# Adjacency counts in groups of 10 targets with three edge chunks, and attention denominators of four chunks summed in eight partitions

## The reference, cut to what matters

```
edge_index = stack([src, dst]); xn = layernorm(x)
# graph layer
norm = dinv[src] * dinv[dst]                       # dinv = 1 / sqrt(degree)
gnn  = relu(segment_sum((xn @ W)[src] * norm[:, None], dst) + b)
# linear attention, 16 heads of 64
phiQ, phiK = elu(Q) + 1, elu(K) + 1
S     = einsum('bhki,bhkj->bhij', phiK, V);  Z = phiK.sum(-2)
denom = einsum('bhqi,bhi->bhq', phiQ, Z)[..., None] + 1e-6
mix   = (einsum('bhqi,bhij->bhqj', phiQ, S) / denom) @ Wo.T + bo
x = x + gnn + mix
x = x + ffn(layernorm(x))                          # ternary weights, silu, two gelu layers
```

## Time and profile before

| | |
|---|---|
| median of 3 runs | 996.22 us (995.83 to 997.37) |
| the profiled execution: its own time | 995.84 us |
| its span in the trace | 994.1 us |
| TensorE busy | 975.2 us, 98% of the span |
| VectorE busy | 543.9 us, 55% |
| ScalarE busy | 293.6 us, 30% |
| GpSimd busy | 142.4 us, 14% |
| granted TensorE clock | 0.999 |

### The profile page before, as it was taken

The page is one execution under the profiler, slowest core; times in us unless marked ns, Lnnn a source line. Parts: engine busy times, 40 slices in busy tenths (PEclk is TensorE's granted clock), DMA queues, the critical chain, the costliest instruction groups (busy, mean ns, idle before and its releaser), DMA issues.

```text
span 994.1 us, 13325 instructions
## 1 busy us (share of the span) xinstructions
PE 975.2 (98%) x4860; PEld 824.4 (83%) x4860; DVE 543.9 (55%) x1067; ACT 293.6 (30%) x585; POOL 142.4 (14%) x191
## 2 busy tenths in 40 slices
PE   5999999999999999999999999999999999999998
PEld 4887888888889989978786788767788999999986
DVE  6886578777763888782113556447557212122354
ACT  6873122232133343341213221114113312135300
POOL 7101001001011050050300000000201103064100
PEclk9999999999999999999999999999999999999999
DMA  7412013113021022122201465535422302010053
GB/s 269 150 49 86 5 30 117 28 31 100 16 77 36 26 90 73 52 69 95 96 12 55 147 204 172 157 119 186 170 80 90 123 1 85 1 43 1 22 190 139
DMA packets 46979, 86.78 MB, mean 87 GB/s; under 512 B 19036, under 2 KB 23388, under 8 KB 46896
## 3 DMA queue, kind: packets, MB, share of 16 engines
q1 hardware_dynamic: 38416, 57.28, 17.5%
q0 software_dynamic: 8480, 28.45, 8.7%
HBM read 61.62 MB, written 24.09 MB: 86 GB/s over the span
## 4 chain that ended last, share of the span: by engine, by line
PE 92%; DVE 3%; DMA 2%; ACT 1%; issue 1%; POOL 1%; SPq 0%; DVEq 0%; ACTq 0%; POOLq 0%
PE PS L1431 11%; PE PS L1433 11%; PE PS L1432 11%; PE PS L1552 9%; PE PS L1553 9%; PE PS L1554 9%; PE PS L1610 5%; PE PS L1612 4%; PE PS L1630 3%; PE PS L1631 3%; PE PS L1629 3%; PE PS L1471 2%; PE PS L1446 2%; PE PS L1683 2%; PE PS L1682 2%; PE PS L1681 2%
## 5 line engine op out<-in xcount | busy, mean ns | idle before, releaser
L1431 PE MATMUL PS<-ring,act_t 128*128 128x512 f32 (+1 forms) x480 | 194.7, 406 | 1.3 <-POOL ring L443 0.6
L1433 PE MATMUL PS<-ring,act_t 128*128 128x512 f32 (+1 forms) x480 | 190.7, 397 | 0.0
L1432 PE MATMUL PS<-ring,act_t 128*128 128x512 f32 (+1 forms) x480 | 190.3, 396 | 0.0
L1552 PE MATMUL PS<-act_t,ring 128*128 128x416 f32 (+1 forms) x432 | 159.3, 369 | 1.4 <-POOL ring L443 1.3
L1553 PE MATMUL PS<-act_t,ring 128*128 128x416 f32 (+1 forms) x432 | 152.2, 352 | 0.0
L1554 PE MATMUL PS<-act_t,ring 128*128 128x416 f32 (+1 forms) x432 | 151.7, 351 | 0.0
L1431 PEld LDWEIGHTS PS<-ring,act_t 128*128 128x128 f32 (+1 forms) x480 | 89.8, 187 | 23.9 <-POOL ring L443 1.6
L1433 PEld LDWEIGHTS PS<-ring,act_t 128*128 128x128 f32 (+1 forms) x480 | 89.5, 186 | 22.4
L1432 PEld LDWEIGHTS PS<-ring,act_t 128*128 128x128 f32 (+1 forms) x480 | 89.9, 187 | 21.2 <-issue 0.5
L1552 PEld LDWEIGHTS PS<-act_t,ring 128*128 128x128 f32 x432 | 81.3, 188 | 6.8 <-issue 3.4
L1553 PEld LDWEIGHTS PS<-act_t,ring 128*128 128x128 f32 x432 | 81.4, 188 | 4.0 <-issue 3.4
(11 more groups left out here) (195 smaller groups left out, 1650.7 us busy)
## 6 DMA issues: line engine op xcount, KB each, us to landing
stage_x<-in_wslices_dram POOLq DMA_DIRECT2D x54, 256.0 KB, 4.2
stage<-in_wslices_dram POOLq DMA_DIRECT2D x42, 256.0 KB, 3.7
xr<-x_d SPq DMA_DIRECT2D x18, 512.0 KB, 3.6
phin_d<-phiq SPq DMA_DIRECT2D x8, 625.0 KB, 3.1
xrow<-in_x_dram SPq DMA_DIRECT2D x9, 512.0 KB, 3.6
xh<-in_x_dram SPq DMA_DIRECT2D x18, 256.0 KB
x_d<-xh SPq DMA_DIRECT2D x18, 256.0 KB
x_d<-xr SPq DMA_DIRECT2D x9, 512.0 KB, 3.0
```

Source lines behind the costliest of these rows:

```text
L1431: pe.matmul(out_ap, node_rows(0, k, t), ring[:, slot(k0 + k), 0, :], start=(k == 0), stop=False)
L1432: pe.matmul(out_ap, node_rows(1, k, t), ring[:, slot(k0 + k), 0, :], start=False, stop=False)
L1433: ins = pe.matmul(out_ap, node_rows(0, k, t), ring[:, slot(k0 + k), 1, :], start=False, stop=(k == KD - 1))
L1552: pe.matmul(out_ap, w[0], x_t[:, 0, k, o:o + n], start=(k == 0), stop=False)
```

## The change

There are two parts.

**Counts.** Groups have 10 targets (`WIN` 13 to 10) and three chunks (`STATIC_CHUNKS` 4 to 3). The first nine tiles then have 13 groups and the last has 10: 127 groups where there were 100. Two groups of a tile that stand beside each other are worked on as a pair (`PARTS`, 68 of them; a tile's thirteenth group stands alone): one pass of VectorE for each of the two arrays, six matmuls into one bank, one copy by ScalarE. Three parts are done in a step, in steps 12 to 34. The array buffers go from 5 to 4 (`OH_BUFS`). The key loads stay one for each group.

**Denominators.** The queries are done in another order (`q_chunk`: for a half of the features, four blocks `f` of one chunk of nodes one after the other). Such a group of four units has its denominators in one PSUM bank, in eight partitions: two heads for each of four units. `z_hl` and `phi_hl` are high and low fp32r parts, so a unit takes three fp32r matmuls with 8 columns of weights (`denominator`), for which ScalarE makes the high part (`phi_split`) and VectorE the low part (`phi_rest`). Once in four units ScalarE copies 8 partitions (`den_copy`) and VectorE inverts them (`den_invert`). SyncE writes them to DRAM (`rec_d`) and reads them back into all 128 partitions, 64 for each head (`rec_spread`). VectorE multiplies unit `i - 8` in its turn `i` (`PHI_LAG`), and each unit is stored by itself.

The core of the diff:

```
-STATIC_CHUNKS = 4
+STATIC_CHUNKS = 3
...
-OH_BUFS = 5
+OH_BUFS = 4
 KEY_BUFS = 4
-WIN = 13
+WIN = 10
...
-PHI_BUFS = 3
+PHI_BUFS = 9
+PHI_LAG = 8
...
+def q_chunk(i):
+
+    s, r = divmod(i, 12)
+    return 4 * s + r % 4, r // 4
...
+def groups_of(t):
+
+    return -(-rows(t) // WIN)
+
+
+PARTS = [(t, j, min(2, groups_of(t) - j)) for t in range(NT) for j in range(0, groups_of(t), 2)]
+
+
 def windows_of(step):
 
-    if 12 <= step < 37:
-        return list(range(4 * (step - 12), 4 * (step - 11)))
+    if 12 <= step < 35:
+        return list(range(3 * (step - 12), min(3 * (step - 11), len(PARTS))))
     return []
...
+            def phin_store(i):
+                f, c = q_chunk(i)
+                o, n = CHUNKS[c]
+                sp.wait_ge(phin_ready, i + 1)
+                sp.dma_start(phin_d[f, :, o:o + n], phiq[:, i % PHI_BUFS, 0:n]).then_inc(phin_stored[i % PHI_BUFS], 16)
+
+            def rec_spread(g):
+                n = CHUNKS[g % 3][1]
+                sp.wait_ge(rec_ready, g + 1)
+                sp.dma_start(rec_d[g].rearrange("a b n -> (a b) n")[:, 0:n], rec[0:8, 0:n]).then_inc(rec_stored, 16)
+                sp.wait_ge(rec_stored, 16 * (g + 1))
+                sp.wait_ge(phin_ready, 4 * g)
+                for h in range(2):
+                    sp.dma_start(rec_all[64 * h:64 * h + 64, :, 0:n],
+                                 rec_d[g, :, h, 0:n].unsqueeze(0).to_broadcast([64, 4, n])).then_inc(rec_in, 16)
...
-                for j in range(WPT):
+                for j in range(groups_of(dt)):
                     w = WPT * dt + j
                     first = sp.value_load(bounds[0:1, w:w + 1], min_val=0, max_val=LAST_FIRST)
...
-                if step >= 40 and (step - 40) % 3 == 2 and (step - 40) // 3 >= 1:
-                    phin_store((step - 40) // 3 - 1)
-            phin_store(KD - 1)
+            for i in range(24 + PHI_LAG):
+                if i >= PHI_LAG:
+                    phin_store(i - PHI_LAG)
+                if 7 <= i < 28 and i % 4 == 3:
...
+            def den_copy(g):
+                n = CHUNKS[g % 3][1]
+                act.wait_ge(phi_used, 4 * (g + 1))
+                if g >= 1:
+                    act.wait_ge(rec_stored, 16 * g)
+                nc.scalar.activation(rec[0:8, 0:n], PS[0:8, 3 + g % 2, 0:n], ACT.Identity,
+                                     bias=eps_sb[0:8]).then_inc(den_read, 1)
+
+            def phi_split(i):
+                n = CHUNKS[q_chunk(i)[1]][1]
+                act.wait_ge(phiq_ready, i + 1)
                 if i >= 2:
-                    act.wait_ge(phin_ready, i - 1)
-                nc.scalar.activation(rec[:, i % 2, 0:n], PS[:, 3 + i % 2, 0:n], ACT.Identity,
-                                     bias=eps_sb).then_inc(den_read, 1)
+                    act.wait_ge(phi_used, i - 1)
+                nc.scalar.activation(phi_hl[:, 0, i % 2, 0:n], phiq[:, i % PHI_BUFS, 0:n], ACT.Copy).then_inc(phi_hi, 1)
...
             def window(w):
-                dt, j = divmod(w, WPT)
+                dt, j, m = PARTS[w]
                 b = w % OH_BUFS
...
+            def phi_rest(i):
+                n = CHUNKS[q_chunk(i)[1]][1]
+                dve.wait_ge(phi_hi, i + 1)
+                dve.tensor_tensor(phi_hl[:, 1, i % 2, 0:n], phiq[:, i % PHI_BUFS, 0:n],
+                                  phi_hl[:, 0, i % 2, 0:n].bitcast(F32), ALU.subtract).then_inc(phi_lo, 1)
+
+            def den_invert(g):
+                n = CHUNKS[g % 3][1]
+                dve.wait_ge(den_read, g + 1)
+                dve.reciprocal(rec[0:8, 0:n], rec[0:8, 0:n]).then_inc(rec_ready, 1)
 
             def den_apply(i):
-                f, c = divmod(i, 3)
-                o, n = CHUNKS[c]
-                dve.wait_ge(rec_ready, i + 1)
-                dve.wait_ge(phiq_ready, i + 1)
-                dve.tensor_tensor(phiq[:, f % PHI_BUFS, o:o + n], phiq[:, f % PHI_BUFS, o:o + n], rec[:, i % 2, 0:n],
+                n = CHUNKS[q_chunk(i)[1]][1]
+                dve.wait_ge(rec_in, 32 * (i // 4 + 1))
+                dve.tensor_tensor(phiq[:, i % PHI_BUFS, 0:n], phiq[:, i % PHI_BUFS, 0:n], rec_all[:, i % 4, 0:n],
                                   ALU.mult).then_inc(phin_ready, 1)
 
             for i in range(24):
                 q_min(i)
-                if i >= 3:
-                    den_invert(i - 3)
+                if i == 1:
+                    z_rest()
+                if i >= 1:
+                    phi_rest(i - 1)
+                if i >= 6 and i % 4 == 2:
+                    den_invert((i - 6) // 4)
+                if i >= PHI_LAG:
+                    den_apply(i - PHI_LAG)
                 q_add(i)
-                if i >= 3:
-                    den_apply(i - 3)
...
-                for j in range(STATIC_CHUNKS):
-                    n = width(w) * NT
-                    ins = pe.matmul(PS[:, b, 0:n], oh_src[:, o, j // 2, :, j % 2], oh_dst[:, o, j // 2, 0:n, j % 2],
-                                    start=(j == 0), stop=(j == STATIC_CHUNKS - 1))
+                _, j, m = PARTS[w]
+                for q in range(STATIC_CHUNKS * m):
+                    i, c = divmod(q, STATIC_CHUNKS)
+                    n = width(j + i) * NT
+                    ins = pe.matmul(PS[:, b, WCOLS * i:WCOLS * i + n], oh_src[:, o, q // 2, :, q % 2],
+                                    oh_dst[:, o, q // 2, 0:n, q % 2], start=(c == 0), stop=(c == STATIC_CHUNKS - 1))
                 ins.then_inc(adj_done, 1)
...
-                for i in range(2):
-                    u = UNIT["z", i]
-                    b = open_unit(u)
-                    for j in range(4):
-                        ins = pe.matmul(PS[:, b, P * j:P * (j + 1)], ksum[:, P * (4 * i + j):P * (4 * i + j + 1)], ones[:],
-                                        start=True, stop=True)
-                    ins.then_inc(acc_full, 1)
+                u = UNIT["z", 0]
+                b = open_unit(u)
+                for f in range(KD):
+                    ins = pe.matmul(PS[:, b, f:f + 1], ksum[:, P * f:P * (f + 1)], ones[:, 0:1], start=True, stop=True)
+                ins.then_inc(acc_full, 1)
...
             def denominator(i):
-                f, c = divmod(i, 3)
-                o, n = CHUNKS[c]
-                for j in range(2):
-                    wait_read(pe, UNIT["z", j])
+                g, j = divmod(i, 4)
+                n = CHUNKS[q_chunk(i)[1]][1]
+                wait_read(pe, UNIT["z", 0])
                 pe.wait_ge(st_ready, 2)
-                pe.wait_ge(phiq_ready, i + 1)
-                if i >= 2:
-                    pe.wait_ge(den_read, i - 1)
-                pe.matmul(PS[:, 3 + i % 2, 0:n], zblk[:, f, :], phiq[:, f % PHI_BUFS, o:o + n],
-                          start=True, stop=True).then_inc(den_done, 1)
+                pe.wait_ge(phi_lo, i + 1)
+                if j == 0 and g >= 2:
+                    pe.wait_ge(den_read, g - 1)
+                for z, b in ((0, 0), (0, 1), (1, 0)):
+                    ins = pe.matmul(PS[0:8, 3 + g % 2, 0:n], z_hl[:, z, i // 12, 8 * j:8 * j + 8], phi_hl[:, b, i % 2, 0:n],
+                                    start=(j == 0 and z + b == 0), stop=(j == 3 and z == 1))
+                ins.then_inc(phi_used, 1)
```

More of the change, by code:

```diff
@@ L151, in sums_of, with width, parts_through @@
     return step + 1 + (step + 1) // NT
-def width(w):
-    return min(WIN, P - w % WPT * WIN)
+def width(j, m=1):
+    return min(WIN * m, P - j * WIN)
+def parts_through(t):
+    return sum(p[0] <= t for p in PARTS)
 def tile_ended(step):
-    return [w // WPT for w in windows_of(step) if w % WPT == WPT - 1]
+    return [PARTS[w][0] for w in windows_of(step) if w + 1 == parts_through(PARTS[w][0])]
 def build(nc, x, src_rows, dst_rows, wslices, wo, bkv, bq, gb, bo, scales, w3s, out):
@@ L1203, in q_add @@
                 wait_read(dve, UNIT["q", f, c])
-                if f >= PHI_BUFS and c == 0:
-                    dve.wait_ge(phin_stored[f % PHI_BUFS], 16 * (f // PHI_BUFS))
-                dve.tensor_tensor(phiq[:, f % PHI_BUFS, o:o + n], qmin[:, i % 2, 0:n], qrel[:, i % 2, 0:n],
+                if i >= PHI_BUFS:
+                    dve.wait_ge(phin_stored[i % PHI_BUFS], 16 * (i // PHI_BUFS))
+                dve.tensor_tensor(phiq[:, i % PHI_BUFS, 0:n], qmin[:, i % 2, 0:n], qrel[:, i % 2, 0:n],
```

165 lines of the change are left out of this document (90 added, 75 removed).

## The result

| | median | range | runs |
|---|---|---|---|
| before | 997.21 us | 995.83 to 997.59 | 5 |
| changed | 1013.87 us | 1012.95 to 1015.69 | 5 |

The ratio is 1.0175 (95% interval 1.0160 to 1.0189): the change costs 16.7 us. I had forecast 997.9 with a range of 992 to 1003. The sum had the direction (+1.7) and a tenth of the size, and of my three outcomes "same" (0.41) stood above "slower" (0.37).

The account below looks back on a forecast made before the run. The prediction took TensorE, busy for 98% of the span, as the bound. Its terms, -5.9 + 2.0 + 6.9 - 3.1 - 0.3 + 2.1 = +1.7 on 995.84, gave 997.5, or 997.9 us as median; range 992 to 1003.

Parts of the forecast that it names:

- Counts, TensorE's own work: Count matmuls on TensorE: fewer columns each would gain 5.9 us, bounds 4.6 to 6.6.
- the line's value: Count matmuls: a line through the times for 130 and 110 columns gives 46 ns for 100; the prediction took 48.
- Key sums: Key sums on TensorE: 16 records with one column in place of 128 would gain 0.3 us.
- (a): Tile 0's keys: 13 loads instead of 10 make the first pairs late, so TensorE waits, +2.0 us.
- (b): Tile 0's store, behind 52 key loads in SyncE's queue, delays ScalarE's copy and TensorE: +6.9 us, bounds 5 to 8.
- Later stores: Count stores after tile 0's: SyncE's queue catches up, so they were counted as 0 (to +1).
- Denominators on TensorE: Three fp32r matmuls take 0.57 us where a denominator took 0.70: -3.1 us over 24, lower bound -4.3.
- Neither is changed: 0: The two changes of slab, 2.2 and 1.3 us of TensorE waiting on GpSimd's subtractions, were expected to stay: 0.
- Rival 2: VectorE's freedom removes 3.5 us at the slab changes and the spread's 2.1 is hidden: 992.3 us, half of it 995; 25%.
- The way through DRAM: Reciprocals stored to DRAM and broadcast back make TensorE wait in groups 1 to 3: +2.1 us, bounds 0 to 6.
- rival 3: The spread is slow, a broadcast from DRAM taking 7 us or more, three groups at 2.5 us: 1003.3 us; 15%.
- four cases: The prediction's three rivals, at 12%, 25% and 15%, and its own forecast of 996 to 1000 us, at 48%.

Follow-up runs that it names:

- e2_den: Only the denominators part of the change, with the counts of the kernel before, run against the kernel before: 1007.48 us, ratio 1.0098.
- e3_store_act: Only the counts part, its ten count stores issued from ScalarE's queue instead of SyncE's, against the kernel before: 994.12 us, ratio 0.9965.
- e4_two_bufs: Denominators part alone, two buffers for spread reciprocals, their store and loads ahead of two stores of finished units, against the kernel before: 1008.34 us, ratio 1.0106.
- the denominators part, even with all its cures: Denominators part alone with two spread buffers, 12 query buffers and the reciprocal ahead of the subtraction, against the kernel before: 998.19 us, ratio 1.0019.

## Why the prediction was wrong

**Counts, TensorE's own work (-5.9).** Right: a count matmul takes 46 ns, the line's value, and the profile gives -5.4 in the steps that can be read without a stall.

**Key sums (-0.3).** Nothing: in e2_den the distance to before is the same, 1.48 us, at the first and at the second query unit.

**(a) Keys of tile 0 (+2.0).** Right: 2.2, at step 13, behind `oh_dst`.

**(b) Store of tile 0 (+6.9, bounds 5 to 8).** Right in mechanism, too small: 11.1, of which 8.6 are the wait. Three sizes were off. The store came at 152.48 and not 150.2: the first load at 94.21 in place of 92.44 (1.4 of that is the later start of the run), 57.44 for the 52 in place of 57.2, and 0.8 from the last load to the store in place of 0.5. ScalarE goes on 3.5 us behind the issue and not 2.2; the earlier trace rows had the median of ten stores, and the first is slower than the others, in the trace of before too, where it landed after 4.1 us. And the low clock behind the stall, 2.5 us, was in no term. e3_store_act shows that all of it goes when the stores stand in another queue.

**Later stores (0).** Right.

**Denominators on TensorE (-3.1).** Right: 0.15 us a unit, so 3.6 for all.

**The step that failed most: "Neither is changed: 0" at the changes of slab.** I had written that VectorE's reciprocals and subtractions leave GpSimd's 1.48 us as they are, since they had done so in the kernel before. They do, for five of six. The first, which begins as VectorE's added subtraction ends, took 4.25. I had looked at each operation's length and not at what stood in front of it and behind it. That is +4.6 at the first change, some 1.6 of it the clock's fall, and +2.2 at the second, 6.8 where I had 0. The table above shows the cost falling with that one subtraction's length, and swapping two of VectorE's calls got about 2.2 us back. Rival 2 expected a gain at this place. I had named the Trainium skill's "SBUF — State Buffer", Who interferes with whom, as speaking against it: an instruction of VectorE with two SBUF inputs contends with GpSimd's reads. The trace bears out that direction and goes further than the sentence: in the changed kernel GpSimd was also held through a reciprocal with one input, when it began as a two-input operation ended.

**The way through DRAM (+2.1, bounds 0 to 6).** The mechanism was right and the size below what came: 2.0 and 3.8 us in two places, and 5.7 in the total with the buffer waits that belong to it. I had 5.0 us from the issue of the first load to the landing of the second; in the two groups that made TensorE wait it was 6.7 and 6.8. That is near rival 3's 7 us; its price of 2.5 a group lies between the two that came, but only two groups paid. What I had missed is the second ring: a store of `phiq` has one turn to land, and my sum had no term for its buffers. The estimate by the Trainium skill's "DMA: Bandwidth & Descriptors", Anatomy of one DMA, of 4.0 us for both loads was too low by the same rows: no single landing was under 4.7. That section is on transfers that GpSimd issues, and these stand in SyncE's queue.

**The chances.** I gave "slower by over 0.2%" 0.37 and had four cases, each with one term gone wrong. What came was three terms off on the same side: +4 at the store, +7 at the changes of slab, +4 at the spread, and 1.3 from the start of the run. They share a part of their cause. Every term was priced as the length of the wait, and three of the waits also cost clock: the store's 2.5 us, the first change of slab some 1.6, the second of the spread's about 1 (0.75 and 0.69 over 434 to 440). The first of the spread's did not (1.00 over 411 to 414).

## What to carry to other kernels

When an edit adds instructions to a queue that issues in order (here 12 loads of 1.10 us), price the next item in it that somebody waits for, and look first whether that item can stand in another queue: moving the stores took back 9 us of the median where the edit's own saving was 5.4. A lag needs two margins, buffers for the result that comes back and buffers for the data that wait; curing one alone shows nothing, as e4_two_bufs did. Taking 34 us off an engine that nobody waits for (VectorE's 543.9 us of busy time are 510.2 in e2_den) gave nothing: the denominators part, even with all its cures, left the kernel about 2 us slower.
